# Mamba inputs beside attention's first maxima, scores in head pairs, expert choice between scan tiles, decays in SBUF

## Chip, cores and metric

One Trainium2 chip; the program runs on 1 of its cores. The metric is the device time of one execution in microseconds (us), the median of the runs. The kernel is written in Bass: every engine has its own program in order, and all waits are semaphores written by hand.

## What is computed

The input is one sequence of 2048 tokens with 128 features. Two layers follow each other; each normalizes its input and adds an "attention" and an "ffn" branch to it.

```python
xn = layernorm(x)
x  = x + long_conv(xn) + token_mix_ffn(xn)           # layer 0
xn = layernorm(x)
x  = x + mamba_both(xn) + attn_moe(xn)               # layer 1, both branches read xn
# mamba_both(x) = x + scan forward + scan backward, 256 inner channels, 16 states each
h = exp(dt[t] * A) * h + (dt[t] * u[t]) * B[t]       # per channel and state
y[t] = sum(h * C[t])                                 # u, z, B, C, dt: projections of xn
# attn_moe(x): 16 heads of 8 features, softmax over 2048 keys; x2 = x + attention;
# then an expert of 8 (argmax of the gate) for each token, hidden size 512, and x2 + expert
```

## The kernel before

**Stages.** The program is a row of stages, each closed by a barrier over all engines: layer 0; attention's preparation (`attention_prep_stage`, L367); attention (`attention_stage`, L467); attention's output (`attention_out_stage`, L788); and the tail (`tail_stage`, L882), which has Mamba and the experts. Time of a tile is never shared over a barrier. The 2048 tokens are cut in 4 chunks of 512 columns (`CH`), and 16 tiles of 128.

**Attention.** Q and K are split in three bf16 parts each, stored in DRAM and loaded again, per group of 4 heads, as stacked rows (L556 to L568): 72 rows (plus 3 for the maxima) with all products for the scores in `qs`/`ks`, and for the odd heads a second copy with 64 rows in `qm`/`km`, which the maxima use. A softmax needs the row maxima before the scores. So the work has two streams. A *maxima job* is two matmuls (an even head at rows 0 to 63, an odd head at rows 64 to 127, L716 and L720) into a ring of three PSUM banks, and DVE reduces each bank to a column (L655). One step (4 heads, 512 queries) has 32 jobs, and there are 16 steps. A *unit* is 128 keys of a step: four score matmuls (L745) into banks 0 to 3, two exponentials on ACT (L634), and the weighing of the values on PE (L758). DVE and PE first run 32 jobs of step 0 and 10 in advance (`LEAD`), and then 256 units, with two jobs beside each as long as there are jobs. POOL splits the maxima (L610 to L616), PE turns them, and SP places them as rows of `qs`.

**Tail.** Mamba's inputs are made chunk by chunk, 8 chunks over both directions: U by 8 matmuls (L1640), Z by 2 (L1644), X by 2 (L1651), D by 2 (L1657); ACT empties the banks and makes silu and the softplus' exp and ln; DVE ends the softplus (L1467) and POOL scales (L1202). They are stored in DRAM and loaded in the layout of the scan. Chunks 0 and 1, the expert choice (L1469 to L1509) and the second normalization stand ahead of the scan loop, the other chunks between its tiles.

The scan loop has 256 tiles (k), 4 to a row r. For a tile ACT writes the decay into one of four PSUM banks (L1346); POOL multiplies the injection, SBUF with SBUF (L1241); DVE scans (L1601), reading the decay from PSUM and the injection from SBUF; then 186 tiles are weighed with C by DVE (L1521, PSUM with SBUF) and 70 by POOL (L1227, from the buffer `hp`), and PE sums them (L1731). POOL may be 4 tiles ahead of the scan (`NI`), ACT 4 (`ND`). The beginning of DVE's tile:

```python
h = decay[k % ND]                      # a PSUM bank
dve.tensor_tensor_scan(h, decay[k % ND], inject[:, k % NI, :], ...)
weigh(k - 1)                           # hc = decay * cs
```

The experts' token scatter, 23 expert slots and gather are spread over the same loop. SP issues almost all DMAs, in order.

Of the kernel before, what the change touches and what calls it, by code (L numbers as in the profile page):

```python
# [67 lines left out]
def layer0_stage(nc, S, dr):  # L68

    with ExitStack() as ctx:  # L70
# [296 lines left out]
def attention_prep_stage(nc, S, dr):  # L367

    with ExitStack() as ctx:
        def sb(name, shape, dt=F32):  # L370
            return ctx.enter_context(nc.sbuf_tensor(name, shape, dt))

        def sem(name):
            return S.enter_sem(nc, name)

        W = sb("ap_w", [P, 3, P])
        bv = sb("ap_bv", [P, P])
        hn = sb("ap_hn", [P, T])
        rem = sb("ap_rem", [P, T])
        parts = sb("ap_parts", [P, 3, T], BF16)  # L380
        banks = S.banks
        w_in, dve_c = sem("ap_w_in"), sem("ap_dve_chain")
        ones_ready, ones_in = sem("ap_ones_ready"), sem("ap_ones_in")
        hn_ready, qk_psum, v_psum = sem("ap_hn"), sem("ap_qk_psum"), sem("ap_v_psum")
        f_ready, hi_ready, v_ready = sem("ap_f"), sem("ap_hi"), sem("ap_v")
        rem1_ready, parts_ready = sem("ap_rem1"), sem("ap_parts_ready")
        stored = [sem("ap_stored_q"), sem("ap_stored_k")]
        block = ctx.enter_context(nc.Block())

        def V(name):  # L390
            return S.vec[:, VCOL[name]:VCOL[name] + 1]

        @block.sync
        def _(sp):
            for i, n in enumerate(("wq", "wk", "wv")):
                sp.dma_start(W[:, i, :], dr[n]).then_inc(w_in, 16)
            sp.dma_start(bv[:, :], dr["bv"]).then_inc(w_in, 16)

            sp.wait_ge(ones_ready, 1)
            for buf in range(2):  # L400
                sp.dma_start(S.ks[DQ:DM, buf, :].rearrange("r (h t) -> r h t", t=T),
                             S.ones[0:3, :].unsqueeze(1).to_broadcast([3, HG, T])).then_inc(ones_in, 16)
            for w in range(2):
                sp.wait_ge(parts_ready, w + 1)
                sp.dma_start(S.qk_dram[w].rearrange("i f t -> f i t"), parts[:, :, :]).then_inc(stored[w], 16)
                sp.wait_ge(stored[w], 16)
            sp.wait_ge(ones_in, 16 * 2)

        @block.gpsimd
        def _(pool):  # L410
            pool.memset(S.ones[:, :], 1.0).then_inc(ones_ready, 1)

        @block.scalar
        def _(act):
            for w, bias in enumerate(("bq", "bk")):
                if w:
                    act.wait_ge(parts_ready, w)
                    act.wait_ge(stored[0], 16)
                for c in range(NCH):
                    act.wait_ge(qk_psum, NCH * w + c + 1)  # L420
                    act.activation(rem[:, c * CH:(c + 1) * CH], banks[4 * w + c][:, :], ACT.Identity,
                                   bias=V(bias)).then_inc(f_ready, 1)
                act.wait_ge(f_ready, NCH * (w + 1))
                act.activation(parts[:, 0, :], rem[:, :], ACT.Copy).then_inc(hi_ready, 1)

        @block.vector
        def _(dve):
            count = [0]

            def link(ins):  # L430
                count[0] += 1
                ins.then_inc(dve_c, 1)
                dve.wait_ge(dve_c, count[0])

            link(dve.tensor_copy(S.identb[:, :], S.ident[:, :]))
            dve.tensor_scalar(hn[:, :], S.xh[:, 0, :], V("ln1_g"), V("ln1_b"), ALU.mult, ALU.add).then_inc(hn_ready, 1)
            for w in range(2):
                dve.wait_ge(hi_ready, w + 1)
                link(dve.tensor_tensor(rem[:, :], rem[:, :], parts[:, 0, :], ALU.subtract))
                link(dve.tensor_copy(parts[:, 1, :], rem[:, :]))  # L440
                dve.tensor_tensor(parts[:, 2, :], rem[:, :], parts[:, 1, :], ALU.subtract).then_inc(parts_ready, 1)
            dve.wait_ge(w_in, 64)
            for c in range(NCH):
                dve.wait_ge(v_psum, c + 1)
                for i in range(TPC):
                    dve.tensor_tensor(S.v[:, :, TPC * c + i, :],
                                      banks[c][:, P * i:P * (i + 1)].rearrange("p (g d) -> p g d", g=NG),
                                      bv[:, :].rearrange("p (g d) -> p g d", g=NG), ALU.add).then_inc(v_ready, 1)

        @block.tensor  # L450
        def _(pe):
            pe.wait_ge(w_in, 64)
            pe.wait_ge(hn_ready, 1)
            for w in range(2):
                for c in range(NCH):
                    pe.matmul(banks[4 * w + c][:, :], W[:, w, :], hn[:, c * CH:(c + 1) * CH],
                              start=True, stop=True).then_inc(qk_psum, 1)
            pe.wait_ge(f_ready, NCH)
            for c in range(NCH):
                for i in range(TPC):  # L460
                    t = TPC * c + i
                    mm = pe.matmul(banks[c][:, P * i:P * (i + 1)], hn[:, P * t:P * (t + 1)], W[:, 2, :],
                                   start=True, stop=True)
                mm.then_inc(v_psum, 1)
# [1406 lines left out]
```

## Time and profile before

| what | us |
|---|---|
| median of 3 runs (lowest, highest) | 1544.89 (1542.99, 1546.82) |
| the profiled execution's own time | 1547.24 |
| its span, first to last instruction | 1545.5 |
| DVE busy | 1255.4 (81%) |
| PE busy | 1117.6 (72%) |
| ACT busy | 896.1 (58%) |
| POOL busy | 499.3 (32%) |
| mean granted TensorE clock | 0.815 of full |

The sums of the parts below are made against the span; what lies around it is 1.7 us. The profiled execution is 2.4 us above the median. The shares of busy time are means over stages with different limits; the chain of waits that ended last names POOL's injection L1241 first, with 8% of the span.

### The profile page before, as it was taken

How to read it: one execution, taken by the hardware profiler on the slowest of the kernel's cores; microseconds unless marked ns; L12 is line 12 of the kernel's file. 1: busy time of each engine (PE TensorE's matmuls, PEld its weight loads, DVE VectorE, ACT ScalarE, POOL GpSimd, SP SyncE). 2: the span in 40 equal slices, each digit the busy share in tenths (PEclk: the TensorE clock that was granted, in tenths of full speed). 3: DMA queues.
4: the chain of work that ended last, by engine and by line, in shares of the span. 5: the costliest groups of instructions: out<-in, count | busy, mean ns of one | idle time of the engine just before them, and what ended most of it. 6: DMA issues, size and time to landing. Idle time of an engine off the chain costs nothing. (4 is left out here: it accounts for less than half of the span.)

```text
span 1545.5 us, 18387 instructions
## 1 busy us (share of the span) xinstructions
PE 1117.6 (72%) x5865; PEld 365.6 (24%) x5865; DVE 1255.4 (81%) x1880; ACT 896.1 (58%) x1315; POOL 499.3 (32%) x460
## 2 busy tenths in 40 slices
PE   1450359999999999999999957556858586546434
PEld 0130002222222222222222224112424242111111
DVE  7952689999999999999999223388877678799996
ACT  3131017777777777777777844547765657556641
POOL 1301000000000000000000000399767677998994
PEclk7765559999999999999999986666868786667565
DMA  1002101000110000000000014658877878756740
GB/s 33 0 10 109 61 32 59 1 1 1 45 45 2 1 19 38 35 1 1 1 1 1 1 34 135 162 125 194 188 202 189 191 192 194 173 120 158 163 100 28
DMA packets 88188, 117.72 MB, mean 76 GB/s; under 512 B 15709, under 2 KB 43140, under 8 KB 88092
## 3 DMA queue, kind: packets, MB, share of 16 engines
q1 hardware_dynamic: 87068, 114.45, 29.0%
q0 software_dynamic: 1024, 2.10, 0.5%
q8 instruction: 47, 0.77, 0.2%
q14 instruction: 49, 0.40, 0.1%
HBM read 90.65 MB, written 25.56 MB: 75 GB/s over the span
## 5 line engine op out<-in xcount | busy, mean ns | idle before, releaser
L655 DVE TENSOR_REDUCE at_mpart<-psum 128x1 f32<-128x512 f32 x1024 | 656.4, 685 | 48.6 <-PE psum L720 38.5
L634 ACT ACTIVATE at_probs<-psum 128x1024 f32<-128x1024 f32 x512 | 496.2, 1021 | 272.1 <-PE psum L745 271.9
L1241 POOL TENSOR_TENSOR t_inject<-t_dus,t_bs 128x512 f32<-128x512 f32 x256 | 322.8, 1281 | 79.4 <-DMA t_dus<-t_dtu_d 60.6
L758 PE MATMUL psum<-at_probs,at_vg 128*32 128x512 f32 x2048 | 273.6, 606 | 0.4 <-ACT at_probs L634 0.4
L745 PE MATMUL psum<-at_qs,at_ks 75*128 75x512 bf16 x1024 | 269.8, 385 | 1.3 <-ACT at_probs L634 0.2
L716 PE MATMUL psum<-at_ks,at_qs 64*128 64x512 bf16 x512 | 207.9, 406 | 83.8 <-DMA at_km<-k_parts 49.5
L610 POOL CAST at_m<-at_mneg 128x16 bf16<-128x16 f32 x16 | 3.1, 196 | 697.5 <-DVE at_mneg L660 697.5
L1731 PE MATMUL psum<-t_hc,t_stack 128*32 128x512 f32 x512 | 102.5, 883 | 173.2 <-DVE t_hc L1521 170.3
L720 PE MATMUL psum<-at_km,at_qm 64*128 64x512 bf16 x512 | 207.9, 406 | 0.0
L1601 DVE TENSOR_TENSOR_SCAN psum<-psum,t_last,t_inject 128x512 f32<-128x512 f32 x132 | 166.3, 1276 | 39.4 <-ACT psum L1346 39.0
L1346 ACT ACTIVATE psum<-t_dts,t_aneg 128x512 f32<-128x512 f32 x256 | 176.6, 694 | 34.9 <-DVE t_hc L1521 23.6
L716 PEld LDWEIGHTS psum<-at_ks,at_qs 64*128 64x128 bf16 x512 | 47.7, 93 | 384.1 <-DVE at_mpart L655 331.3
L1521 DVE TENSOR_TENSOR t_hc<-psum,t_cs 128x512 f32<-128x512 f32 x186 | 124.0, 667 | 0.0
L745 PEld LDWEIGHTS psum<-at_qs,at_ks 75*128 75x128 bf16 x1024 | 78.2, 98 | 135.4 <-issue 52.1
L1227 POOL TENSOR_TENSOR t_hc<-t_hp,t_cs 128x512 f32<-128x512 f32 x70 | 88.8, 1268 | 18.5 <-DVE t_hp L1601 18.5
L1640 PE MATMUL psum<-t_xm,t_taps 128*128 128x512 f32 x128 | 71.5, 713 | 23.7 <-DVE t_taps L1461 14.0
L1601 DVE TENSOR_TENSOR_SCAN t_hp<-psum,t_last,t_inject 128x512 f32<-128x512 f32 x60 | 76.1, 1268 | 13.0 <-issue 7.5
L1358 ACT ACTIVATE t_last<-psum 128x1 f32<-128x1 f32 x142 | 24.2, 171 | 104.1 <-DVE t_hc L1521 102.8
L1601 DVE TENSOR_TENSOR_SCAN psum<-psum,t_inject 128x512 f32<-128x512 f32 x54 | 65.8, 1224 | 20.4 <-POOL t_inject L1241 15.3
L1731 PEld LDWEIGHTS psum<-t_hc,t_stack 128*32 128x32 f32 x512 | 14.1, 128 | 241.1 <-issue 235.8
L758 PEld LDWEIGHTS psum<-at_probs,at_vg 128*32 128x32 f32 x2048 | 40.4, 108 | 63.4 <-issue 61.7
L720 PEld LDWEIGHTS psum<-at_km,at_qm 64*128 64x128 bf16 x512 | 47.7, 93 | 0.0
(242 smaller groups left out, 994.2 us busy)
## 6 DMA issues: line engine op xcount, KB each, us to landing
t_dts<-t_dt_d SPq DMA_DIRECT2D x64, 256.0 KB, 5.6
t_dus<-t_dtu_d SPq DMA_DIRECT2D x64, 256.0 KB, 9.2
t_w<-in_w SPq DMA_DIRECT2D x46, 256.0 KB
t_bs<-t_bc_d SPq DMA_DIRECT2D x128, 64.0 KB
t_cs<-t_bc_d SPq DMA_DIRECT2D x128, 64.0 KB
at_qs<-q_parts SPq DMA_DIRECT2D x48, 96.0 KB
at_ks<-k_parts SPq DMA_DIRECT2D x48, 96.0 KB
t_u_d<-t_u SPq DMA_DIRECT2D x8, 512.0 KB, 3.1
```

The costliest lines, as they stand in the source:

```text
L634: act.activation(probs[:, u % 2, p, :], s_pair[p], ACT.Exp, scale=float(HD) ** -0.5).then_inc(probs_ready, 1)
L655: dve.reduce_max(mpart[:, s % 2, 2 * jp + b, i, kc:kc + 1], ring[x % 3], AX.X).then_inc(ring_free, 1)
L716: pe.matmul(ring[x % 3], S.qs[0:HALF, buf, q], S.ks[0:HALF, buf, k], start=True, stop=True)\
L720: pe.matmul(ring[y % 3], S.qm[64:64 + HALF, buf, q], S.km[64:64 + HALF, buf, k], start=True, stop=True)\
L745: mm = pe.matmul(s_banks[p][b], S.ks[0:DM, g % 2, j * T + kt * P:j * T + (kt + 1) * P], S.qs[0:DM, g % 2, j * T + c * CH:j * T + (c + 1) * ...
L758: mm = pe.matmul(o_bank[VW * j:VW * (j + 1), :], vg[:, g % 2, kt, j, :], probs[:, u % 2, j // 2, CH * (j % 2):CH * (j % 2 + 1)], start=(kt ...
L1227: pool.tensor_tensor(hc[:, r % 2, j, :], hp[:, by_pool[k] % NHP, :], cs[:, (NQ * (i // NB) + q) % NBC, :], ALU.mult).then_inc(pool_weighed, 1)
L1241: pool.tensor_tensor(inject[:, k % NI, :], dus[:, i % 2, j, :], bs[:, m % NBC, :], ALU.mult).then_inc(injected, 1)
L1346: act.activation(decay[k % ND], dts[:, i % 2, j, :], ACT.Exp, scale=aneg[:, n // NCH, m:m + 1])\
L1521: dve.tensor_tensor(hc[:, r % 2, j, :], decay[k % ND], cs[:, m % NBC, :], ALU.mult).then_inc(dve_weighed, 1)
L1601: dve.tensor_tensor_scan(h, decay[k % ND], inject[:, k % NI, :], last[:, k % PC:k % PC + 1] if n % NCH else 0.0, ALU.mult, ALU.add).then_i ...
L1731: mm = pe.matmul(y_bank[GC * j:GC * (j + 1), :], stack[:, :], hc[:, r % 2, j, :], start=False, stop=(q == NQ - 1), tile_position=(0, GC * j))
```

## The change

- **One front stage.** `attention_prep_stage` and `attention_stage` become `front_stage`. All of its weights are loaded in layer 0. The parts of Q and K are made by chunks.
- **Mamba's inputs in the front.** The 56 steps of the 8 chunks (16 U, 16 Z, 8 X, 16 D) are made in banks 0 to 3: 16 of them ahead of the maxima, 40 one each before the first 40 of the 42 early jobs. ACT applies silu straight from PSUM. POOL scales the taps and the inputs; all is stored to DRAM from the front.
- **Scores in pairs.** The score rows fall from 75 to 59 (56 and 3 for the maxima): an even head at rows 0 to 58, an odd head at rows 64 to 122, side by side, and `qm`/`km` go. The maxima use 56 rows of the same tiles. A group's loads fall from 36 to 24.
- **Output in the tail.** `attention_out_stage` becomes the tail's beginning; its bias is added by POOL in the front (L664), and constants (`diag`, `stack`, `aneg`) are made there.
- **Choice between tiles.** Normalization, logits, choice and places of the tokens run on DVE and PE between the first 39 scan tiles; scatter moves from rows 0 to 3 to rows 10 to 13, the first expert slot from row 8 to 17, the gather from row 36 to 46.
- **Decays in SBUF.** ACT writes the decays into `spread`, six SBUF buffers, and DVE scans and weighs from there. The number of tiles weighed by POOL stays 70.

```diff
-        ND, NI, NHP, NBC = 4, 4, 3, 5
-        FIRST_SLOT = 8
-        GATHER = 36
+        ND, NI, NHP, NBC = 6, 4, 3, 5
+        FIRST_SLOT = 17
+        GATHER = 46
+        SCATTER = 10
...
-        decay, y_bank, ring = S.banks[0:ND], S.banks[ND], S.banks[ND + 1:8]
+        spread = sb("spread", [P, ND, CH])
+        y_bank, ring = S.banks[4], S.banks[5:8]
+        decay = [spread[:, i, :] for i in range(ND)]
...
-                for b in range(2):
-                    j = 2 * p + b
-                    mm = pe.matmul(s_banks[p][b], S.ks[0:DM, g % 2, j * T + kt * P:j * T + (kt + 1) * P],
-                                   S.qs[0:DM, g % 2, j * T + c * CH:j * T + (c + 1) * CH], start=True, stop=True)
+                for b in range(2):
+                    mm = pe.matmul(s_banks[p][b], ks[half(b, DM), g % 2, of_pair(p, kt * P, P)],
+                                   qs[half(b, DM), g % 2, of_pair(p, c * CH, CH)], start=True, stop=True)
...
+            for n in range(JOBS + LEAD):
+                if n < len(beside):
+                    step(beside[n])
+                if n == JOBS:
+                    turn_max(0)
+                maxima(n)
...
+            both(store_uz, 0)
+            for w in range(2):
+                sp.wait_ge(stored[w], 16 * NCH)
+            for j in range(HG):
+                load(0, j)
...
+                if 2 <= k < 2 + NCH:
+                    attended_out(k - 2)
+                    standardize(k - 2)
+                if k == 24:
+                    for c in range(NCH):
+                        logits(c)
+                if k == 25:
+                    choose()
+                if 36 <= k < 39:
+                    place[k - 36]()
```

The order of DVE at the first scan tiles, before (`t_dt` and `t_soft` are the softplus, psum in L1601 is a decay bank):

```order
L1507 TENSOR_REDUCE t_eidf<-t_passed 128x23
L1508 TENSOR_SCALAR t_eidf<-t_eidf 128x23
L1509 CAST t_eid<-t_eidf 128x23
L1467 TENSOR_TENSOR t_dt<-t_dt,t_soft 128x1024
L1601 SCALAR_TENSOR_TENSOR psum<-psum,t_inject 128x512 x2
L1521 TENSOR_TENSOR t_hc<-psum,t_cs 128x512
```

The same place on DVE in the changed kernel (`t_spread` is the decay, `t_hp` the buffer of POOL's tiles):

```order
L1515 BN_AGGR t_mv<-t_st 128x2 x16
L1517 TENSOR_SCALAR t_lnv<-t_mv 128x16
L1533 SCALAR_TENSOR_TENSOR t_hp<-t_spread,t_inject 128x512
L1533 SCALAR_TENSOR_TENSOR t_spread<-t_spread,t_inject 128x512 x2
L1456 TENSOR_TENSOR t_hc<-t_spread,t_cs 128x512
L1390 TENSOR_TENSOR res<-res,xn 128x512
L1486 TENSOR_SCALAR xn<-xn,t_mv,t_rstd 128x128 x4
```

The choice and the softplus are gone from ahead of the first tile; the scan and the weighing name two SBUF tiles where one was psum; the normalization follows the third tile.

PE from the projections to the first maxima, before:

```order
L456 MATMUL psum<-ap_hn,ap_w 128x512 x8
L462 MATMUL psum<-ap_w,ap_hn 128x128 x16
L369 UNCONDITIONAL_BRANCH
L701 UNCONDITIONAL_BRANCH
L716 MATMUL psum<-at_ks,at_qs 128x512
L720 MATMUL psum<-at_km,at_qm 128x512
```

And in the changed kernel (`mp_taps` gives U, `mp_w_in` Z, `mp_w_x` X; L915 is a maxima job):

```order
L965 MATMUL psum<-at_vg,w_qkv 128x512 x8
L888 MATMUL psum<-mp_xm,mp_taps 128x512 x8
L892 MATMUL psum<-mp_xm,mp_w_in 128x512 x2
L972 MATMUL psum<-w_qkv,at_vg 128x128 x16
...
L896 MATMUL psum<-mp_u,mp_w_x 40x512 x2
L915 MATMUL psum<-at_ks,at_qs 128x512 x2
```

The branches (a stage's end) are gone, U and Z of the first four chunks stand ahead of the first job (three more times the two rows L888 and L892 where the line of dots is), and then a step and a job alternate.

## Rows read from the trace of the kernel before

**Rows 1.** Stages: us; busy (count) of PE, PEld, DVE, ACT, POOL; clock, DMA share, GB/s.

```profile
98.80:138.90 40.10, 13.45 (x48) 7.78 (x48) 17.97 (x24) 8.99 (x10) 1.77 (x1) 0.65 0.23 88
138.90:164.10 25.20, 0.00 (x0) 0.00 (x1) 0.00 (x0) 0.00 (x0) 4.99 (x4) 0.50 0.18 72
164.10:224.00 59.90, 25.68 (x85) 4.50 (x85) 53.21 (x84) 0.00 (x0) 0.83 (x4) 0.50 0.09 37
224.00:905.40 681.40, 674.63 (x4093) 171.74 (x4091) 615.30 (x1005) 504.03 (x528) 13.62 (x62) 0.99 0.04 15
905.40:996.40 91.00, 56.27 (x164) 30.57 (x164) 31.04 (x109) 37.55 (x48) 11.22 (x16) 0.66 0.44 121
996.40:1529.00 532.60, 311.13 (x1347) 129.19 (x1347) 455.68 (x491) 316.12 (x691) 447.69 (x359) 0.71 0.69 162
```

**Rows 2.** Timeline near 602 us: start, us, engine, line, operation.

```profile
601.21 5.06 DVE L655 TENSOR_REDUCE at_mpart<-psum 128x1 f32<-128x512 f32 x8
602.27 1.04 PE L745 MATMUL psum<-at_qs,at_ks 75*128 75x512 bf16 x4
604.88 1.04 PE L745 MATMUL psum<-at_qs,at_ks 75*128 75x512 bf16 x4
```

**Rows 3.** Timeline, PE and ACT in the last units, near 885 us.

```profile
885.01 1.04 PE L745 MATMUL psum<-at_qs,at_ks 75*128 75x512 bf16 x4
885.71 3.91 ACT L634 ACTIVATE at_probs<-psum 128x1024 f32<-128x1024 f32 x4 [0.32 <-PE psum L745]
889.23 1.04 PE L745 MATMUL psum<-at_qs,at_ks 75*128 75x512 bf16 x4
```

**Rows 4.** Groups of instructions by line, 996.4 to 1529 us: count, busy, mean ns, idle before.

```profile
L1241 POOL TENSOR_TENSOR t_inject<-t_dus,t_bs 128x512 f32<-128x512 f32 x253 | 319.0, 1281 | 56.3 <-DMA t_dus<-t_dtu_d 37.7 <-DVE psum L1601 16.1 <-DMA t_cs<-t_bc_d 1.5
L1521 DVE TENSOR_TENSOR t_hc<-psum,t_cs 128x512 f32<-128x512 f32 x186 | 124.0, 667 | 0.0
L1467 DVE TENSOR_TENSOR t_dt<-t_dt,t_soft 128x1024 f32<-128x1024 f32 x6 | 11.6, 1927 | 0.0
L1440 DVE TENSOR_TENSOR res<-res,xn 128x512 f32<-128x512 f32 x4 | 5.8, 1444 | 0.0
L1440 DVE TENSOR_TENSOR res<-res,psum 128x512 f32<-128x512 f32 x4 | 2.7, 666 | 0.0
```

**Rows 5.** Timeline, POOL and DVE near 1478 us: decays from PSUM.

```profile
1477.27 2.45 DVE L1601 TENSOR_TENSOR_SCAN psum<-psum,t_last,t_inject 128x512 f32<-128x512 f32 x2
1478.07 4.94 POOL L1241 TENSOR_TENSOR t_inject<-t_dus,t_bs 128x512 f32<-128x512 f32 x4
1479.63 0.67 DVE L1521 TENSOR_TENSOR t_hc<-psum,t_cs 128x512 f32<-128x512 f32 x1
1480.22 1.27 DVE L1601 TENSOR_TENSOR_SCAN psum<-psum,t_last,t_inject 128x512 f32<-128x512 f32 x1
```

**Rows 6.** Timeline, POOL and DVE at 1380 us: a DVE operation with two SBUF inputs.

```profile
1380.35 1.26 POOL L1227 TENSOR_TENSOR t_hc<-t_hp,t_cs 128x512 f32<-128x512 f32 x1 [1.82 <-DVE t_hp L1601]
1380.77 1.92 DVE L1467 TENSOR_TENSOR t_dt<-t_dt,t_soft 128x1024 f32<-128x1024 f32 x1
1381.57 2.24 POOL L1241 TENSOR_TENSOR t_inject<-t_dus,t_bs 128x512 f32<-128x512 f32 x1
```

**Rows 7.** Timeline, layer 0: POOL beside a scan whose inputs are both in SBUF.

```profile
53.74 4.46 DVE L270 TENSOR_TENSOR_SCAN l_whole<-l_sc,l_pim 128x2048 f32<-128x2048 f32 x1
53.99 8.09 POOL L155 TENSOR_TENSOR l_kact<-l_kact 128x512 f32<-128x512 f32 x2 [33.46 <-ACT l_kact L180]
```

**Rows 8.** Lines L846 and L848, POOL idle: ns least, median, most.

```profile
L846 DVE TENSOR_TENSOR xn<-xn,psum x4: 677/680/689, 911.3 to 917.4; 128x512 f32<-128x512 f32 x4
L848 DVE TENSOR_TENSOR xn<-xn,ao_bo x4: 691/691/691, 912.0 to 918.1; 128x512 f32<-128x512 f32 x4
```

**Rows 9.** Groups by line, 920.2 to 996.4 us: PE's part of two chunks.

```profile
L1640 PE MATMUL psum<-t_xm,t_taps 128*128 128x512 f32 x32 | 19.4, 774 | 14.0 <-DVE t_taps L1461 14.0
L1644 PE MATMUL psum<-t_xm,t_w_in 128*128 128x512 f32 x8 | 3.8, 592 | 0.0
```

More of the change, by code:

```diff
@@ L361 @@
 HG = NH // NG
-DQ = 9 * HD
+DQ = 7 * HD
 DM = DQ + 3
 VW = 32
[L367 to L464, printed above, removed]
@@ L581, in _ @@
+            for p in range(2):
+                both(store_bc, p)
+                both(store_dt, p)
+                both(store_dtu, p)
+                both(store_uz, p + 2)
             place_max(0)
+            for p in range(2, NP):
+                both(store_bc, p)
+                both(store_dt, p)
+                both(store_dtu, p)
             for j in range(HG):
                 load(1, j)
+            for t, n in ((S.wo[:, :], "wo"), (S.gw[:, :], "gate_w"), (S.gb[:, :], "gate_b")):
+                sp.dma_start(t, dr[n]).then_inc(late_in, 16)
@@ new lines, in softened @@
+            def softened(p):
+                for n in (2 * p, 2 * p + 1):
+                    act.wait_ge(prep_free, USE["D", n, NB - 1] + 1)
+                    act.activation(soft[:, n % 4, :, :], soft[:, n % 4, :, :], ACT.Exp, scale=-1.0).then_inc(exp_ready, 1)
+                for n in (2 * p, 2 * p + 1):
+                    act.wait_ge(exp_ready, n + 1)
+                    act.activation(soft[:, n % 4, :, :], soft[:, n % 4, :, :], ACT.Ln, bias=1.0).then_inc(ln_ready, 1)
+            for w in range(2):
+                for c in range(NCH):
+                    queries_keys(w, c)
@@ new lines, in softplus @@
+            def softplus(n):
+                dve.wait_ge(prep_free, USE["D", n, NB - 1] + 1)
+                dve.wait_ge(ln_ready, n + 1)
+                dve.tensor_tensor(dt[:, n % 4, :, :], dt[:, n % 4, :, :], soft[:, n % 4, :, :], ALU.add).then_inc(dt_ready, 1)
+            for c in range(NCH):
+                dve.tensor_scalar(hn[:, cols(c)], S.xh[:, 0, cols(c)], V("ln1_g"), V("ln1_b"), ALU.mult, ALU.add).then_inc(hn_ready, 1)
+            normed_input(0)
+            normed_input(1)
+            for w in range(2):
+                for c in range(NCH):
+                    parts_of(w, c)
@@ new lines, in _ @@
+            for c in range(NCH):
+                dve.wait_ge(v_psum, c + 1)
+                dve.tensor_tensor(S.v[:, :, TPC * c:TPC * (c + 1), :],
+                                  S.banks[4 + c].rearrange("p (i g d) -> p g i d", i=TPC, g=NG),
+                                  S.bv[:, :].rearrange("p (g d) -> p g d", g=NG).unsqueeze(2).to_broadcast([P, NG, TPC, HG * HD]),
+                                  ALU.add).then_inc(v_ready, 1)
+            normed_input(2)
+            normed_input(3)
@@ L692, in _ @@
+            for u_ in range(NU):
+                s, kt = divmod(u_, NT)
+                for n in jobs_beside(u_, 0):
                     maxima(n)
@@ L761, in weigh @@
                 mm.then_inc(weighed, 1)
[L763 to L769 removed]
+            for w in range(2):
+                for c in range(NCH):
+                    if w == 0:
+                        pe.wait_ge(hn_ready, c + 1)
+                    pe.matmul(S.banks[4 * w + c], S.w_qkv[:, w, :], hn[:, cols(c)], start=True, stop=True).then_inc(qk_psum, 1)
@@ new lines, in _ @@
+            for key in STEPS[:4]:
+                step(key)
+            for c in range(NCH):
+                pe.wait_ge(f_ready, NCH + c + 1)
+                for i in range(TPC):
+                    t = TPC * c + i
+                    mm = pe.matmul(S.banks[4 + c][:, P * i:P * (i + 1)], hn[:, P * t:P * (t + 1)], S.w_qkv[:, 2, :],
+                                   start=True, stop=True)
+                mm.then_inc(v_psum, 1)
+            for key in STEPS[4:ALONE]:
+                step(key)
@@ L1212, in gather @@
                 if i == 0:
[L1213 to L1214 removed]
+                    pool.wait_ge(y_st, 16 * NSLOT)
                     pool.wait_ge(scattered, 16 * NT)
```

936 lines of the change are left out of this document (433 added, 503 removed).

## The prediction, made before the changed kernel was run

> **What bounds the kernel now.** I read the stages first [rows 1]. The unit loop takes 681.4 us, and DVE works 615.3 of it. The timeline near 602 us shows why: eight reductions take 5.06 us, 0.632 each, and four of them go with a unit, which comes every 2.61 us (602.27 to 604.88) [rows 2]. DVE's reductions bound that loop. PE looks as full (674.6), but in the last 20 or so units, which have no maxima beside them, two units take 4.22 us, and ACT's four exponentials fill 3.91 of it [rows 3]. So ACT's floor is 1.95 a unit and PE's is lower than 2.61. Ahead of the loop stand 65.3 us from layer 0's end (98.8) to the first maxima (164.1), 25.2 of which only loads fill, and 59.9 us of 42 early jobs. Behind it stand 91.0 us of output, Mamba's first inputs and choice, in which no engine but PE is over half busy, and 532.6 us of scan loop with DVE at 455.7 and POOL at 447.7 [rows 1]. The last figure decides: two engines, both near 85%, work side by side.
>
> Then I asked what lets them. Near 1478 us two scans take 2.45 us and a weighing 0.67, while POOL's four injections run through at 4.94, 1.235 each [rows 5]. There each DVE operation has one input in PSUM. Where DVE has two SBUF inputs it is another picture. In the scan loop `res<-res,xn` takes 1444 ns, `res<-res,psum` of the same size 666; the softplus' product takes 1927 [rows 4], and 1225 where POOL is idle [rows 9]. At 1380.77 it starts beside POOL's multiplication, which ends at 1381.61; it ends at 1382.69, 1.08 us later. POOL's next operation starts in between and ends at 1383.81, 1.12 after that [rows 6]. Each waited the other out in full. In layer 0, a scan with both inputs in SBUF runs 53.74 to 58.20, and two POOL operations beside it take 8.09 us [rows 7], against 1.24 for one of their size in [rows 5]. The source alone costs nothing: with POOL idle an addition takes 680 ns with an input from PSUM and 691 with both from SBUF [rows 8]. This is the Trainium skill's rule too, page "SBUF — State Buffer", section "Who interferes with whom": a DVE instruction with two SBUF inputs contends with a GpSimd instruction that reads SBUF, the first one keeps the shared port pair to its end, and with one SBUF input there is no contention. By that rule, rows 4 to 7 agree.
>
> **The change, part by part**, against the span of 1545.5.
>
> *First maxima, −16.* The two preparations' barriers go. PE needs 13.45 us for Q, K and V [rows 1] and now does chunks 0 and 1 among them. A chunk's U and Z are 16 and 4 instructions; 0.61 and 0.47 each in [rows 9] at mixed clocks. I take 0.47 for all, since PE is busy without a break, so 9.4 a chunk (0.61: 12). That gives 98.8 + 13.5 + 18.8 = 131.1. SP issues the store of chunk 1's Z ahead of the loads and so waits until then. A group's loads, 25.2 us at 72 GB/s before, shrink to 12 with some 0.9 MB: 12.5 us at that rate, with issue and landing to 147. PE does chunks 2 and 3 meanwhile and ends at 150. First maxima at 148, bounds 142 and 160. The 19 weight loads that moved into layer 0 lie beside its 98.8 us of DVE work and cost nothing; without that cover they would cost the front a few microseconds.
>
> *Early jobs, +30.* 42 jobs took 59.9, 1.43 each. Of 40 steps, 8 are U (8 instructions of 0.47 and the job's own 0.5: 4.3), 8 are X (4: 2.4), and the Z and D steps (0.94) hide below 1.43. 8 x 4.3 + 8 x 2.4 + 26 x 1.43 = 91, less 1 for what the three-bank ring evens out: 90. DVE's softplus and bias work and POOL's scalings and stores run beside PE-bound jobs. Bounds 72 (all steps hidden but U's) and 115 (PE at the lower of its two levels in part of it, as it was, 0.50, in the stage before [rows 1]).
>
> *Unit loop, −6.* Scores in pairs take PE's 1.04 [rows 2] to about half, but DVE's four reductions stay at 2.53 to 2.61. Only the last 20 units gain, 2.11 to 1.95, 3 us, and the loop's beginning some 5 with a busier PE; the last softplus operations cost 2. Bounds −20 and +10.
>
> *Output and prologue, −71.* Of 91.0 us, about 20 stay: four additions (0.69 each [rows 8], with PE's part some 6 us), while SP issues the 14 `dts`, `dus`, Z and `bc` loads for the first row; at the 25.2 us that 18 of attention's loads took with their landing [rows 1], 1.4 each, that is 20. The choice, 2 chunks' preparation and the first normalization are gone from the path. They lie now in the scan loop or in the early jobs. SP's queue is where this could fail: the place stores and the attention output's loads stand in one queue with the first row's. Bounds 15 and 32.
>
> *Scan loop, +257.* All 256 scans and 186 weighings now have two SBUF inputs; POOL's 256 injections and 70 weighings always did. If they exclude each other, their times add: scans 1.18 apart and a weighing 0.59 (1477.27, 1479.63, 1480.22 [rows 5]): 256 x 1.18 + 186 x 0.59 + 326 x 1.235 = 302 + 110 + 403 = 815. An operation that waits with its head start hides some of its own beginning: 1.08 and 1.12 in [rows 6] against 1.14 (1225 less the 0.08 overlap) and 1.235. All waiting gives 815 − 442 x 0.06 − 326 x 0.11 = 752. Middle 783, and 7 for DVE's other operations that meet POOL. 790, 3.1 us a tile; bounds 740 and 835. The two further buffers (six decays, not four) buy ACT slack that is not on the path: ACT is at 316 of 532.6 [rows 1]. Choice and normalization on DVE, some 25 us, run while POOL holds DVE's other work off only in part; that is inside the bounds. POOL's 37.7 us of waiting for the `dus` loads [rows 4] vanish beneath. The last 16.5 us stay.
>
> The Trainium skill, page "VectorE: DVE Perf Modes", section "The TRN2 errata — SBUF-src ops pay a fixed extra latency per instruction", gives DVE 58 cycles of fixed cost from SBUF and 120 from PSUM at 0.96 GHz: an estimate of 65 ns less for each of the 442 operations, 29 us, and by it the sum would be 1709; [rows 8] show 11 ns more, not 65 less, so the row decides.
>
> Sum: 1545.5 − 16 + 30 − 6 − 71 + 257 = 1739.5. What lies around the span adds 1.7, and the median is 2.4 below this execution: **1738 us**.
>
> **Rivals.**
>
> *A: no exclusion for the scan* (faster). It may be that the port is taken by `tensor_tensor` alone, or per element instead of per instruction, so that DVE and POOL go on side by side. The scan loop begins at 996.4 − 16 + 30 − 6 − 71 = 933. With DVE at 456 and the choice's 25 less the softplus' 12, it would be about 475: 933 + 475 + 16.5 − 0.7 = 1424. The point that decides is 596 us for the loop, the 532.6 of before plus the 63 saved ahead of it: with under 0.47 us of mutual waiting a tile the change wins. For it speaks only that rows 6 show a `tensor_tensor`; against it [rows 7], where the DVE operation is a scan. Chance 0.10.
>
> *B: PE falls to the lower level in the unit loop* (slower still). The granted clock is 0.99 there (2.4 GHz), and was 0.50 (1.2 GHz) in the early jobs, where PE worked 25.7 us of 59.9 [rows 1]. Pairs cut PE's work by 0.52 of 2.61 a unit. If the level fell in half of the loop, PE's 2.1 a unit would become 3.6 to 4.2 and bound: 128 x 1 to 1.5, some +120 at least, about 1860. Against it: with 2.1 of 2.6 PE is still far busier than in the early jobs, and the last 20 units, without maxima, kept 2.11 [rows 3]. Chance 0.05.
>
> *C: the steps beside the early jobs don't overlap* (the change's first part does not do what it says): PE at the lower level there, 0.94 an instruction for the 16 U and X steps, 96 instructions: +45, about 1783. Chance 0.13, within the range.
>
> **How the numbers follow.** The forecast has 0.72, C 0.13, A 0.10, B 0.05. The range takes in the forecast and C and the bounds of the scan loop, −50 and +45, with part of the others: 1670 to 1805. A measurement of this kernel can tell 0.3%, 4.6 us, from no change; hardly any case lies there: faster 0.11 (A and a little), same 0.01, slower 0.88.
>
> **What would show it.** In the changed kernel's profile: scans and injections with mean durations of 2 us and more where they were 1.23 and 1.28, and DVE's and POOL's busy times together about 1500 in a loop of 790, overlapping though only one of them works; first maxima near 148; units from about 238 on, 2.6 apart, at clock 1.0; the first scan some 20 us after the last unit, near 933. The forecast is wrong if injections keep 1.24 to 1.28 beside scans (then A), if units stand over 3 us apart (B), or if the early jobs take over 120 us (C).

## The result: 1739.21 us, and the profile after

The changed kernel takes 1739.21 us, median of 4 runs (1736.69 to 1740.83), against 1545.86 for the kernel before in the same comparison (4 runs). The ratio is 1.1243 with a 95% interval of 1.1203 to 1.1283: 12% slower. The forecast was 1738, in a range of 1670 to 1805.

The profiled execution has a span of 1735.9 us, 190.4 more than before. By stage, in the form of [rows 1] (stretch, length, busy time and count on PE, weight loads, DVE, ACT, POOL, then clock, DMA share, GB/s):

```profile
98.80:154.70 55.90, 48.23 (x132) 22.64 (x132) 30.45 (x41) 21.54 (x34) 11.55 (x7) 0.94 0.37 130
154.70:254.30 99.60, 94.26 (x228) 27.81 (x229) 60.74 (x92) 58.87 (x78) 17.52 (x10) 0.84 0.35 129
254.30:911.90 657.60, 556.51 (x4089) 124.93 (x4085) 598.48 (x1005) 509.36 (x535) 27.19 (x74) 0.99 0.04 14
911.90:937.50 25.60, 9.50 (x60) 7.37 (x60) 9.88 (x47) 9.67 (x15) 2.90 (x10) 0.69 0.76 144
937.50:1719.50 782.00, 282.00 (x1231) 132.88 (x1231) 759.83 (x522) 245.60 (x587) 632.51 (x357) 0.57 0.41 95
```

Set beside the forecast:

| part | before | forecast change | after | change |
|---|---|---|---|---|
| layer 0's end to first maxima | 65.3 | −16 | 55.9 | −9.4 |
| 42 early jobs | 59.9 | +30 | 99.6 | +39.7 |
| unit loop | 681.4 | −6 | 657.6 | −23.8 |
| output to first scan | 91.0 | −71 | 25.6 | −65.4 |
| scan loop | 532.6 | +257 | 782.0 | +249.4 |
| end | 16.5 | 0 | 16.4 | −0.1 |

The total is right partly by luck, because misses cancel: 6.6, 9.7, −17.8 and 5.6 us ahead of the loop and −7.6 in it, −3.6 in all with the end. What is left of this cancels too: the forecast took the median as 2.4 us below the profiled execution, and it came 1.6 above. The scan loop is the large term, and its groups (line, operation, count, busy us, mean ns, idle before) are to be set beside [rows 4]:

```profile
L1278 POOL TENSOR_TENSOR t_inject<-t_dus,t_bs 128x512 f32<-128x512 f32 x255 | 465.6, 1843 | 84.4 <-DVE t_spread L1533 47.0 <-DMA t_dus<-mp_dtu_d 23.9 <-issue 12.8
L1533 DVE TENSOR_TENSOR_SCAN t_spread<-t_spread,t_last,t_inject 128x512 f32<-128x512 f32 x142 | 311.7, 2212 | 0.0
L1456 DVE TENSOR_TENSOR t_hc<-t_spread,t_cs 128x512 f32<-128x512 f32 x186 | 201.4, 1083 | 0.0
L1265 POOL TENSOR_TENSOR t_hc<-t_hp,t_cs 128x512 f32<-128x512 f32 x70 | 120.7, 1724 | 51.1 <-DVE t_hp L1533 48.8 <-DMA t_cs<-mp_bc_d 2.3
```

An injection has gone from 1281 to 1843 ns, a weighing on DVE from 667 to 1083, and a scan, 1.27 us in [rows 5], to 2.21. DVE and POOL are together "busy" for 1392 us in 782, since both count while one waits for the other. The timeline of the two shows the turns. A scan that takes 1.27 us in [rows 5] is drawn out to 2.2 or 2.3, and POOL's two injections to 4.31:

```profile
1308.08 2.28 DVE L1533 TENSOR_TENSOR_SCAN t_spread<-t_spread,t_last,t_inject 128x512 f32<-128x512 f32 x1
1309.24 4.31 POOL L1278 TENSOR_TENSOR t_inject<-t_dus,t_bs 128x512 f32<-128x512 f32 x2
1310.29 2.21 DVE L1533 TENSOR_TENSOR_SCAN t_hp<-t_spread,t_last,t_inject 128x512 f32<-128x512 f32 x1
```

### The profile page after: what moved, and what is told of

It reads as the page before. It is cut to its first block and busy times, and to the rows that moved or that the text cites. A ratio compares the mean times of both kernels' runs of the same rounds, so it can differ in the third digit from the quotient of the medians.

```text
span 1735.9 us, 18239 instructions
## 1 busy us (share of the span) xinstructions
PE 1029.7 (59%) x5865; PEld 339.0 (20%) x5865; DVE 1541.7 (89%) x1874; ACT 874.5 (50%) x1286; POOL 710.5 (41%) x472
## 5 line engine op out<-in xcount | busy, mean ns | idle before, releaser
L1278 POOL TENSOR_TENSOR t_inject<-t_dus,t_bs 128x512 f32<-128x512 f32 x256 | 466.8, 1841 | 104.0 <-DVE t_spread L1533 47.0
L1644 PE MATMUL psum<-t_hc,stack 128*32 128x512 f32 x512 | 123.1, 1052 | 405.7 <-DVE t_hc L1456 405.7
L1533 DVE TENSOR_TENSOR_SCAN t_spread<-t_spread,t_last,t_inject 128x512 f32<-128x512 f32 x142 | 311.7, 2212 | 0.0
L915 PE MATMUL psum<-at_ks,at_qs 56*128 56x512 bf16 x1024 | 203.3, 394 | 93.5 <-DVE at_mpart L768 92.8
L1336 ACT ACTIVATE t_spread<-t_dts,aneg 128x512 f32<-128x512 f32 x256 | 183.0, 723 | 87.0 <-DVE t_hc L1456 50.7
L1456 DVE TENSOR_TENSOR t_hc<-t_spread,t_cs 128x512 f32<-128x512 f32 x186 | 201.4, 1083 | 0.0
L943 PE MATMUL psum<-at_qs,at_ks 59*128 59x512 bf16 x1024 | 158.1, 380 | 9.7 <-ACT at_probs L744 8.2
L915 PEld LDWEIGHTS psum<-at_ks,at_qs 56*128 56x128 bf16 x1024 | 49.3, 93 | 425.6 <-DVE at_mpart L768 410.0
L1533 DVE TENSOR_TENSOR_SCAN t_hp<-t_spread,t_last,t_inject 128x512 f32<-128x512 f32 x50 | 102.1, 2041 | 11.5 <-POOL t_inject L1278 8.4
L1533 DVE TENSOR_TENSOR_SCAN t_spread<-t_spread,t_inject 128x512 f32<-128x512 f32 x44 | 89.3, 2048 | 0.0
L888 PE MATMUL psum<-mp_xm,mp_taps 128*128 128x512 f32 x128 | 60.5, 621 | 0.0
```

Of the source, the lines that this page charges most:

```text
L888: mm = pe.matmul(out, S.taps[:, d, i, P * b:P * (b + 1)], xm[:, n % 2, i:i + CH], start=(i == 0), stop=(i == KC - 1))
L915: pe.matmul(ring[z_ % 3], qs[half(b, DQ), buf, of_pair(jp, c * CH + i * P, P)], ks[half(b, DQ), buf, of_pair(jp, kc * CH, CH)], start=True ...
L943: mm = pe.matmul(s_banks[p][b], ks[half(b, DM), g % 2, of_pair(p, kt * P, P)], qs[half(b, DM), g % 2, of_pair(p, c * CH, CH)], start=True, ...
L1278: pool.tensor_tensor(inject[:, k % NI, :], dus[:, i % 2, j, :], bs[:, m % NBC, :], ALU.mult).then_inc(injected, 1)
L1336: act.activation(decay[k % ND], dts[:, i % 2, j, :], ACT.Exp, scale=S.aneg[:, n // NCH, m:m + 1])\
L1456: dve.tensor_tensor(hc[:, r % 2, j, :], decay[k % ND], cs[:, m % NBC, :], ALU.mult).then_inc(dve_weighed, 1)
```

## The experiments

All loop lengths below run from the start of the first scan to that of the last gating (the multiplication of a finished row with `t_uz`), in the profiled execution of each kernel. The stage above ends 2.1 us earlier. By the measure used here, the loop is 784 us in the changed kernel and 535 in the kernel before.

**Decays back in PSUM.** In the changed kernel:

```diff
-        ND, NI, NHP, NBC = 6, 4, 3, 5
+        ND, NI, NHP, NBC = 4, 4, 3, 5
-        decay = [spread[:, i, :] for i in range(ND)]
+        decay = S.banks[0:ND]
```

> The changed kernel with its decays in four PSUM banks, as before, and all else kept. Mutual exclusion of DVE and POOL (theory): scans take 1.23 us and weighings 0.67 again, injections 1.24 to 1.3; the scan loop falls from 782 us to 470 to 530, the total to 1425 to 1485 us. Rival: the loop is long because choice, normalization and scatter now lie in it and the experts start later: then it stays over 650 us and the total over 1600.

Measured: 1494.23 us, ratio 0.9654 (0.9616 to 0.9691); the loop is 539 us. The groups of the loop:

```profile
L1277 POOL TENSOR_TENSOR t_inject<-t_dus,t_bs 128x512 f32<-128x512 f32 x256 | 320.3, 1277 | 93.9 <-issue 37.7 <-DMA t_dus<-mp_dtu_d 28.6 <-DMA t_cs<-mp_bc_d 20.3
L1532 DVE TENSOR_TENSOR_SCAN psum<-psum,t_last,t_inject 128x512 f32<-128x512 f32 x142 | 178.8, 1277 | 12.0 <-issue 9.2 <-ACT psum L1335 2.6
L1455 DVE TENSOR_TENSOR t_hc<-psum,t_cs 128x512 f32<-128x512 f32 x186 | 124.0, 667 | 0.0
```

Every duration is back at the value of before. Decays in SBUF cost 245 us, in the loop and in the total; all the other parts of the change together gain 3.5%. The total and the loop each missed their range by 9 us: I had set the loop by DVE's and POOL's work and left out idle time, of which POOL's row shows 93.9. This version also has four decay buffers and not six. The number is not the cause: the kernel with the scans alone (below) has four in SBUF, and its scans are slow.

**Half of it in the kernel before.** Buffers 0 and 1 of the four in SBUF:

```diff
-        decay, y_bank, ring = S.banks[0:ND], S.banks[ND], S.banks[ND + 1:8]
+        spread = sb("spread", [P, 2, CH])
+        decay = [spread[:, 0, :], spread[:, 1, :]] + S.banks[2:ND]
+        y_bank, ring = S.banks[ND], S.banks[ND + 1:8]
```

> The kernel before with two of its four decay buffers in SBUF (tiles 0 and 1 of each row) and two in PSUM, nothing else changed. Exclusion: 128 scans and 64 weighings shut POOL out, 128 x 1.18 + 64 x 0.59 = 189 us, on top of POOL's 403 of its own: loop at least 592, about 620 against 532.6, total 1605 to 1665. Rival, the place of the decays costs nothing by itself: total within 0.3% of 1545.

Measured: 1636.82 us, ratio 1.0567 (1.0503 to 1.0631), inside the range of the exclusion; the loop is 628 us. Which scans are slow follows the buffer. Groups by line and shape, part of the loop:

```profile
L1603 DVE TENSOR_TENSOR_SCAN psum<-psum,t_last,t_inject 128x512 f32<-128x512 f32 x84 | 106.9, 1272 | 11.2 <-ACT psum L1348 11.2
L1603 DVE TENSOR_TENSOR_SCAN t_hp<-t_spread,t_last,t_inject 128x512 f32<-128x512 f32 x48 | 97.9, 2040 | 4.7 <-issue 4.7
```

The same line takes 1272 ns with a PSUM input and 2040 with two from SBUF, in one loop. So nothing else of the change is needed for the effect.

**Scan and weighing apart.** In one kernel the scan's inputs are both in SBUF but its result goes to PSUM, so that the weighing has one SBUF input. In the other the decays come from PSUM and the result goes to SBUF, so that only the weighing has two. Both have four decay buffers; ACT, which copies a tile's last column, follows the result's place in both (not shown).

```diff
-                    h = decay[k % ND]
+                    h = S.banks[k % 4]
...
-                dve.tensor_tensor(hc[:, r % 2, j, :], decay[k % ND], cs[:, m % NBC, :], ALU.mult)
+                dve.tensor_tensor(hc[:, r % 2, j, :], S.banks[k % 4], cs[:, m % NBC, :], ALU.mult)
```

> The changed kernel with four SBUF decay buffers, but a scan of a DVE tile writes its state to a PSUM bank, so that its weighing has one SBUF input; the scans keep two. Exclusion per instruction: scans 302 us and POOL's 403 exclude each other, weighings do not: loop about 705 less the 4% that waiting operations hide, 680, with stalls up to 710; total 1635 to 1665. Rival, the weighing alone causes the loss (the scan does not take the port): loop near 540 as with all decays in PSUM, total about 1495.

```diff
-        decay = [spread[:, i, :] for i in range(ND)]
+        decay = S.banks[0:ND]
...
-                    h = decay[k % ND]
+                    h = spread[:, k % ND, :]
...
-                dve.tensor_tensor(hc[:, r % 2, j, :], decay[k % ND], cs[:, m % NBC, :], ALU.mult)
+                dve.tensor_tensor(hc[:, r % 2, j, :], spread[:, k % ND, :], cs[:, m % NBC, :], ALU.mult)
```

> The changed kernel with decays in four PSUM banks, but the states written to SBUF, so that a scan has one SBUF input and the 186 weighings two. Exclusion: 110 us of weighings on top of POOL's 403 is 513, and the stalls at block borders of about 80 stay: loop 560 to 620, total 1515 to 1575. Rival, a result in SBUF blocks POOL too: then as slow as the changed kernel, 1739.

Measured: 1647.67 us (ratio 1.0672, 1.0625 to 1.0719), loop 692; and 1548.49 us (1.0028, 1.0006 to 1.005), loop 592. DVE's groups of the first and then of the second:

```profile
L1533 DVE TENSOR_TENSOR_SCAN psum<-t_spread,t_last,t_inject 128x512 f32<-128x512 f32 x142 | 257.9, 1831 | 17.3 <-issue 12.2 <-ACT t_spread L1336 5.0
L1456 DVE TENSOR_TENSOR t_hc<-psum,t_cs 128x512 f32<-128x512 f32 x186 | 123.4, 664 | 0.0
```

```profile
L1456 DVE TENSOR_TENSOR t_hc<-t_spread,t_cs 128x512 f32<-128x512 f32 x186 | 208.9, 1123 | 0.0
L1533 DVE TENSOR_TENSOR_SCAN t_spread<-psum,t_last,t_inject 128x512 f32<-128x512 f32 x142 | 179.6, 1270 | 0.6
```

Each instruction is slow exactly where both of its inputs are in SBUF. A result in SBUF does nothing: 1270 ns a scan here, 1277 in the PSUM version. This ends rival A in the form that only `tensor_tensor` takes the port: the scans alone cost 153 us over the 539 of the PSUM version, the weighings alone 53. Both together cost 245, so the parts do not simply add.

**Less work on POOL.** If only the sum of both engines' times counts, work is better done by the one that needs less for it. First all weighings on DVE, then the injections too:

```diff
-            return not SCATTER <= r < SCATTER + 4 and not GATHER <= r < GATHER + 4 and (j == 0 or j == 2 and r % 4 == 1)
+            return False
```

> The changed kernel with all 256 weighings on DVE, none on POOL; decays in SBUF. Exclusion: only the sum of both engines' holds counts, and 70 weighings fall from about 1.2 us on POOL to 0.6 on DVE: 42 us less, total about 1696. Rival, DVE is only slowed by SBUF operands (2.1 us a scan, 1.08 a weighing) and is the bound: 70 x 1.08 = 76 us more, total about 1815.

```diff
-                pool.tensor_tensor(inject[:, k % NI, :], dus[:, i % 2, j, :], bs[:, m % NBC, :], ALU.mult)
...
+            injection(0)
             for k in range(NK):
...
+                if k + 1 < NK:
+                    injection(k + 1)
                 dve.wait_ge(decay_ready, k + 1)
```

> The changed kernel with all injections and weighings on DVE; POOL only scatters and gathers. Exclusion: with nobody to wait for, a scan takes 1.2 us, a multiplication 0.6: 256 x (1.18 + 0.59 + 0.59) = 604, and some 45 for the rest: loop about 650, total about 1605, faster than with POOL's help. Rival, slowed by SBUF operands alone: 256 x (2.1 + 1.08 + 1.08), total over 2000.

Measured: 1721.00 us (ratio 1.111, 1.1056 to 1.1165), loop 770; and 1630.74 us (1.0528, 1.0477 to 1.0578), loop 678. Both are faster than with POOL's help. Slower SBUF operands alone can't give that; by that rival both would be slower. Two of DVE's groups in the second:

```profile
L1541 DVE TENSOR_TENSOR_SCAN t_spread<-t_spread,t_last,t_inject 128x512 f32<-128x512 f32 x192 | 244.6, 1274 | 0.0
L1450 DVE TENSOR_TENSOR t_hc<-t_spread,t_cs 128x512 f32<-128x512 f32 x256 | 169.4, 662 | 0.0
```

With POOL silent, a scan from SBUF takes 1274 ns and a weighing 662, as from PSUM (1277, 667). The sizes were off by some 25 us each. The first gained 18 and not 42. The sum of holds there (a hold is the time in which one engine keeps the other out), by the spacings of [rows 5], is 256 x (1.18 + 0.59 + 1.235) = 769, and the loop is 770, whereas the changed kernel's loop is 31 under its 815. That the first meets its sum so closely is in part chance, since DVE is busy for only 734.9 us of it. The second has 604 us of such work and stands at 678. DVE is idle for 49.8 us before its injections, 34.8 of them for loads; the 45 us that I had set for everything else did not cover that.

**POOL in the front.** In the front stage PE starts 6.7 us behind DVE's first operation. The timeline of the changed kernel there:

```profile
99.74 1.79 POOL L648 MEMSET at_ones<- 3x2048 bf16 x1 [30.52 <-POOLq L59]
99.78 6.63 DVE L823 TENSOR_SCALAR at_vg<-xh,vec 128x512 f32<-128x512 f32 x1 [7.78 <-PEq L59]
101.50 4.62 POOL L620 TENSOR_TENSOR mp_taps<-mp_taps,mp_w_in 128x1024 f32<-128x1024 f32 x2
106.47 2.07 PE L965 MATMUL psum<-at_vg,w_qkv 128*128 128x512 f32 x2 [8.30 <-DVE at_vg L823]
```

DVE's first operation ends 0.3 us after POOL's last. Only one of its inputs is a tensor in SBUF, `xh`; `vec` holds a column of factors. In the PSUM version PE starts 6.7 us behind it as well. To that version one wait was added:

```diff
+            pool.wait_ge(hn_ready, NCH)
             scaled_taps(0)
             scaled_taps(1)
```

> As e1_psum, and POOL scales the taps only after DVE has made the four chunks of the first input. Exclusion: DVE's first tensor_scalar there took 6.63 us beside POOL's 2.33 us multiplications; it falls to below 1 us, PE starts some 6 us earlier, first maxima at 148 to 150, total 5 to 6 us under e1_psum (1488). Rival, the wait is not for POOL: no change at PE's start.

```profile
98.70 1.79 POOL L648 MEMSET at_ones<- 3x2048 bf16 x1 [29.88 <-POOLq L59]
98.74 3.40 DVE L824 TENSOR_SCALAR at_vg<-xh,vec 128x512 f32<-128x512 f32 x4 [7.13 <-PEq L59]
100.83 2.93 PE L966 MATMUL psum<-at_vg,w_qkv 128*128 128x512 f32 x3 [3.70 <-DVE at_vg L824]
```

PE starts 2.1 us behind DVE's first operation instead of 6.7; it has 4.6 us back, and the first maxima come at 149.3, in the range expected. But DVE's first operation still takes 2.03 us and not under 1: POOL's memset, which stayed ahead of the wait, ends 0.3 us before it. The total is 1489.77 (ratio 0.9644, 0.9611 to 0.9677), whose interval overlaps that of the version without the wait, so the gain is shown by the timeline and not by the total.

**Clock in the early jobs.** The first D steps of the changed kernel, with a job before each, are slower from the third on, which starts at 159.96:

```profile
158.59 1.12 PE L900 MATMUL psum<-mp_bcx,mp_w_dt 8*128 8x512 f32 x2
159.96 1.47 PE L900 MATMUL psum<-mp_bcx,mp_w_dt 8*128 8x512 f32 x2
161.90 2.07 PE L900 MATMUL psum<-mp_bcx,mp_w_dt 8*128 8x512 f32 x2
```

Below are two windows of this kernel. The first has the last of these D steps and the U step behind them, the second U, Z and X steps and the start of the next D steps. Over 162 to 166 us the clock is at its lower level, 0.50:

```profile
161.00:170.00 9.00, 9.00 (x18) 3.01 (x18) 2.96 (x6) 7.21 (x10) 0.00 (x0) 0.64 0.14 55
170.00:194.00 24.00, 24.00 (x66) 7.67 (x66) 16.95 (x26) 10.65 (x15) 5.56 (x2) 1.00 0.36 135
```

The D steps were then given 128 rows:

```diff
-                    mm = pe.matmul(out, S.w_dt[BC:BC + DR, d, P * b:P * (b + 1)], bcx[BC:BC + DR, n % 2, :], start=True, stop=True)
+                    mm = pe.matmul(out, S.w_in[:, d, P * b:P * (b + 1)], S.xh[:, d, (n % NCH) * CH:(n % NCH + 1) * CH], start=True, stop=True)
```

> As e1_psum, but the D steps multiply 128 rows (of another input) in place of 8; their results are therefore not dt's. If the granted clock of the early jobs falls behind the D steps because so few rows work there, it stays at the upper level, the 99.6 us of early jobs fall to 86 to 90 and the total by about 10 us against e1_psum. Rival, the clock falls with the pauses and bf16 jobs: no change.

Early jobs of this kernel, then those of the PSUM version that it was made from:

```profile
155.20:245.40 90.20, 84.43 (x228) 25.91 (x229) 60.34 (x92) 57.84 (x77) 17.52 (x10) 0.96 0.37 138
```

```profile
156.40:256.10 99.70, 93.52 (x226) 28.24 (x227) 60.66 (x92) 59.09 (x78) 17.52 (x10) 0.84 0.35 129
```

The granted clock is 0.96 in place of 0.84 and the stage 9.5 us shorter, at the upper end of what was expected (86 to 90). PE is busy for all of both stretches above (9.00 of 9.00, 24.00 of 24.00), so pauses are not what lowers the clock there; with 8 rows replaced by 128 in the D steps it stays at 1.00 up to 226 us. It then falls to 0.65 over 226 to 230 us, and there PE had just waited 1.7 us for POOL. The edit changes the input's values along with the rows, and no run parts the two. The total is 1488.50 (0.9646, 0.9612 to 0.9681); of the 10 us expected, the spans show 7 and the totals cannot tell it.

**Why the unit loop gained 24 us.** Units are 2.49 us apart after, 2.61 before. My first theory was the pairs:

```diff
-                    mm = pe.matmul(s_banks[p][b], ks[half(b, DM), g % 2, of_pair(p, kt * P, P)],
-                                   qs[half(b, DM), g % 2, of_pair(p, c * CH, CH)], start=True, stop=True)
+                    mm = pe.matmul(s_banks[p][b], ks[half(0, DM), g % 2, of_pair(p, kt * P, P)],
+                                   qs[half(0, DM), g % 2, of_pair(p, c * CH, CH)], start=True, stop=True)
```

> As e1_psum, but both score matmuls of a pair use the same 59 rows (the even head's, so that odd heads' scores are wrong), and can't run side by side. If the unit loop before was bound by PE at 2.61 us a unit and the pairs removed that, PE has 2.0 + 0.5 again: units 2.55 to 2.61 apart in place of 2.49, loop 672 to 682 in place of 657, total 12 to 25 us over e1_psum (1506 to 1519). Rival, DVE's reductions bounded the loop before and still do: units stay 2.49 apart, total as e1_psum.

Measured: 1498.18 us (0.9687, 0.9651 to 0.9723). The timeline of PE:

```profile
606.25 1.06 PE L956 MATMUL psum<-at_probs,at_vg 128*32 128x512 f32 x8
607.25 0.39 PE L915 MATMUL psum<-at_ks,at_qs 56*128 56x512 bf16 x2
607.47 1.03 PE L943 MATMUL psum<-at_qs,at_ks 59*128 59x512 bf16 x4
608.42 0.39 PE L915 MATMUL psum<-at_ks,at_qs 56*128 56x512 bf16 x2
608.74 1.06 PE L956 MATMUL psum<-at_probs,at_vg 128*32 128x512 f32 x8
```

The scores take 1.03 us again, one after the other, and the units stay 2.49 apart: the theory fell. (The total is 4 us over that of the PSUM version, with intervals that overlap.) But the scores begin 0.22 us after the job (607.25 to 607.47), and in the kernel before 0.32:

```profile
601.95 0.39 PE L716 MATMUL psum<-at_ks,at_qs 64*128 64x512 bf16 x1
601.95 0.39 PE L720 MATMUL psum<-at_km,at_qm 64*128 64x512 bf16 x1
```

(the scores follow at 602.27 [rows 2]). A job's matmuls use rows 0 to 63 and 64 to 127. A weight load of 75 rows covers rows of both halves, one of 59 rows only of the first. So the number of rows was cut in the kernel before:

```diff
-                    mm = pe.matmul(s_banks[p][b], S.ks[0:DM, g % 2, j * T + kt * P:j * T + (kt + 1) * P],
-                                   S.qs[0:DM, g % 2, j * T + c * CH:j * T + (c + 1) * CH], start=True, stop=True)
+                    mm = pe.matmul(s_banks[p][b], S.ks[0:59, g % 2, j * T + kt * P:j * T + (kt + 1) * P],
+                                   S.qs[0:59, g % 2, j * T + c * CH:j * T + (c + 1) * CH], start=True, stop=True)
```

> The kernel before, whose score matmuls use rows 0 to 58 in place of 0 to 74 (16 rows of the scores, maxima among them, are left out, and the exponential's scale is made small so that it stays finite); the four score matmuls still run one after the other. Theory: the unit loop before was bound by PE at 2.61 us, because a weight load of 75 rows has to wait for both halves of the array, 0.09 us more behind a job; with 59 rows it starts beside the odd head's matmul: units 2.49 to 2.53 apart, 19 to 28 us less, total 1518 to 1527. Rival, DVE's reductions bounded it and the gain of 24 us in the changed kernel has another cause: total within 0.3% of 1546.

Measured: 1522.94 us (ratio 0.984, 0.98 to 0.9879), in the range of the theory. PE's matmuls, then its weight loads, and last the same load in the kernel before:

```profile
602.44 1.06 PE L758 MATMUL psum<-at_probs,at_vg 128*32 128x512 f32 x8
603.43 0.39 PE L716 MATMUL psum<-at_ks,at_qs 64*128 64x512 bf16 x1
603.66 1.02 PE L745 MATMUL psum<-at_qs,at_ks 59*128 59x512 bf16 x4
604.93 1.07 PE L758 MATMUL psum<-at_probs,at_vg 128*32 128x512 f32 x8
```

```profile
603.43 0.09 PEld L720 LDWEIGHTS psum<-at_km,at_qm 64*128 64x128 bf16 x1
603.45 0.74 PEld L745 LDWEIGHTS psum<-at_qs,at_ks 59*128 59x128 bf16 x4
```

```profile
602.26 0.55 PEld L745 LDWEIGHTS psum<-at_qs,at_ks 75*128 75x128 bf16 x4 [0.23 <-issue]
```

Units are 2.49 apart (602.44 to 604.93). The scores' first load starts 0.02 us behind the job's loads, while the job's matmuls run; the load of 75 rows in the kernel before starts 0.31 us behind the start of the job's matmuls (601.95 to 602.26). The gain of the unit loop comes from fewer rows, not from the pairs. What in the array lets the shorter load start earlier is not shown, only that it does. DVE's four reductions, 0.62 each, are probably the next bound at 2.49, for in the PSUM version PE waits 0.35 us for one of them in a unit; so the shorter time of a pair brings nothing.

**A version that beats both.** In the PSUM version SP waits 41.9 us for PE (to free an expert's weights) in front of the block loads that ACT and POOL need. SP's waits there (in all, times, longest):

```profile
SPq L1170 <- ACT psum L1335: 61.2, 7, 24.1
SPq L1194 <- PE psum L1611: 41.9, 7, 10.0
```

```diff
-                if (s := slot_at(r, -4)) is not None:
+                if (s := slot_at(r, -2)) is not None:
                     load_expert(s)
```

> As e6_taps (decays in PSUM, taps later), and SP issues an expert's weights two rows ahead in place of four, so that it doesn't sit waiting for PE (41.9 us in e1_psum) in front of the block loads that POOL and ACT wait for. If SP's order causes the stalls at block borders: 10 to 30 us off, total 1460 to 1480. Rival, the transfers themselves take that long (DMA share 0.72): no change from 1490.

And with the weights loaded two rows ahead:

```profile
SPq L1171 <- ACT psum L1336: 58.6, 6, 24.2
SPq L1195 <- PE psum L1612: 5.4, 1, 5.4
```

Measured: 1456.33 us, ratio 0.9414 (0.9375 to 0.9453), 33 us under the same kernel with the loads four rows ahead, a little more than expected. The loop is 507 us, where the PSUM version has 539 and the kernel that this one was made from 541. POOL's idle time before injections that is put down to no release ("issue") falls from 39.8 to 3.4; what it waits for loads stays (46.7 and 49.5). So the 33 us came from the queue's order and not from the transfers.

## Why the prediction was right, and where it was not

**What bounds the kernel.** For the tail the reading held: two engines work side by side as long as each DVE operation has one SBUF input. One of its figures, 1225 ns for the softplus' product with POOL idle, is not in [rows 9] as the text has it; the timeline has it:

```profile
956.01 1.22 DVE L1467 TENSOR_TENSOR t_dt<-t_dt,t_soft 128x1024 f32<-128x1024 f32 x1 [15.80 <-ACT t_soft L1298]
```

For the unit loop it failed. I wrote that DVE's reductions bound it at 2.61; eight in 5.06 us is 0.632 each and 2.53 a unit, so 0.08 a unit was unexplained, while PE's row showed 674.63 of 681.4 [rows 1]. PE was the bound.

**First maxima** (−16, came −9.4, in the bounds). Two steps failed. The forecast let the loads decide, at 148, although by its own costs PE has the four chunks and an X step ahead of the first job: 98.8 + 13.5 + 4 x 9.4 + 1.9 = 151.8. And PE starts 7.7 us after layer 0's end, where the forecast had nothing; 4.6 of them are POOL's tap scaling, which holds DVE's first operation up. Q, K and V and the four chunks then took 4.7 us less than costed, which gives 154.8. The trace has PE in this order without a wait:

```profile
151.08 1.88 PE L892 MATMUL psum<-mp_xm,mp_w_in 128*128 128x512 f32 x4
152.89 1.91 PE L896 MATMUL psum<-mp_u,mp_w_x 128*40 128x512 f32 x4
154.74 0.39 PE L915 MATMUL psum<-at_ks,at_qs 56*128 56x512 bf16 x2
```

**Early jobs** (+30, came +39.7). With the clock at 0.96 the stage takes 90.2, and the forecast was 90. What failed is the clock, a part of rival C: 0.84 on the mean, with the fall in and behind D steps, not in all of the U and X steps, and 9.5 us in place of 45.

**Unit loop** (−6, came −23.8, outside its bounds of −20 and +10). The term "the four reductions stay at 2.53 to 2.61" was wrong: PE's four scores and their loads bounded the loop at 2.61, and 59 rows in place of 75 take 0.12 off that, with pairs or without.

**Output and prologue** (−71, came −65.4). The first injection starts at 936.09 behind the first `cs` load, 24 us after the last unit, and the first scan at 937.5. Some 3 us of the 5.6 that were missed pass before the tail issues its first load at 914.99; the rest are issues and landings on SP's queue.

**Scan loop** (+257, came +249.4). The sum of holds comes within 4%. Sum against loop: 815 and 784 for the changed kernel, 705 and 692 with the scans alone, 769 and 770 with all weighings on DVE. Where the sum falls under what the loop needs otherwise, it stops to count: 513 and 592 with the weighings alone, where the PSUM version needs 539.

**Rivals.** A is refuted for scans and for weighings by a run each. B did not come: granted 0.99 in the unit loop, although PE is busy for 556.5 of 657.6. The decision point of A, 596 us for the loop, is borne out from the other side. By the terms as they came, 58.9 us were saved ahead of the loop, so the point is 535 + 58.9 = 594 by the measure of the experiments. The kernel with the weighings alone has its loop at 592 and stands at 1548.49, level with the one before.

**Fixed cost of SBUF operands.** The Trainium skill, page "VectorE: DVE Perf Modes", section "The TRN2 errata — SBUF-src ops pay a fixed extra latency per instruction", has DVE's fixed cost lower from SBUF than from PSUM by 62 cycles. No run here shows it: with POOL silent, 1274 against 1277 ns for the scan and 662 against 667 for the weighing. The rule on shared ports, page "SBUF — State Buffer", section "Who interferes with whom", agrees with all of the runs on scans and weighings: slow with two SBUF inputs, not slow with one, whatever the place of the result. It frees an instruction with one SBUF input only outside the modes in which DVE uses both of its ports, and it counts `tensor_scalar` among the operations that can enter them; the prediction left that condition out. It would cover the front's first `tensor_scalar`, which POOL held up with one tensor from SBUF, but no run here shows in which mode that one ran.

## What to carry to other kernels

Before an operand of a DVE instruction is moved from PSUM to SBUF, count its SBUF inputs: with two, its time adds to POOL's instead of running beside it, and then POOL's help can cost more than it brings. One SBUF input is no warrant for every operation: scans and weighings with one ran freely, a `tensor_scalar` did not. When two engines both look full, take the period of the loop and subtract each one's own work; the one that leaves nothing is the bound. And of a long queue on SP, look at what it waits for in front of the loads that the bound engines need.

## What was not expected of the hardware

- POOL can keep its turn over consecutive instructions: a `tensor_scalar` that takes 0.53 us a little later waited out a memset and two multiplications, 6.63 us in all, and the memset alone when the multiplications were moved (2.03 us). That a turn is not offered between them was seen in the front alone.
- Behind two half-array matmuls, a weight load of 59 rows starts 0.02 us after theirs, one of 75 rows 0.31 us after they start: 0.23 against 0.32 us from job to scores, and 23 us of the kernel before, for 16 rows fewer.
- In a stretch of matmuls of 8 rows and the U step behind them the granted clock was 0.64 over 9 us, though PE had no pause; with 128 rows (and other values) in their place it stayed at 1.00 there.
- Two SBUF inputs cost nothing with POOL silent: 1274 against 1277 ns for a scan.
